# Roll stage of the third attention: norm's power for two batches, counts on VectorE and tags on ScalarE

## What is computed

```python
agg = jnp.einsum('bhekl,bk->bhel', gathered, tmp_corr)      # rolled values, weighted
out = agg.transpose(0, 3, 1, 2).reshape(Bq, Lq, Dq) @ Wo + bo
x = x + jnp.tanh(g_xattn[3]) * out
xn = _layernorm(x)                                           # (x - mean) / sqrt(var + 1e-5)
logits = jnp.einsum('bsh,eh->bse', xn, Wr)                   # 8 experts
top_v, top_i = jax.lax.top_k(jax.nn.softmax(logits), 2)      # two experts for each token
```

## Time and profile before

| | us |
|---|---|
| median of 3 runs | 1148.77 |
| lowest, highest | 1145.1, 1150.56 |
| the profiled run | 1153.46 |
| its span in the trace | 1151.7 |

### The profile page before, as it was taken

How to read it: one execution, slowest core, us unless ns; L and a number is a source line. 1 busy time by engine, 2 the same in 40 slices (tenths; PEclk the granted TensorE clock), 3 DMA queues, 4 the chain that set the end, 5 groups by cost and what they waited for, 6 DMA issues and landing times. The chain is left out here.

```text
span 1151.7 us, 21666 instructions
## 1 busy us (share of the span) xinstructions
PE 882.2 (77%) x6156; PEld 647.7 (56%) x6156; DVE 657.5 (57%) x1975; ACT 503.8 (44%) x1403; POOL 459.5 (40%) x835
## 2 busy tenths in 40 slices
PE   0799994788379999999649996799967727429992
PEld 0265663677247777777526775476655616317771
DVE  1588993434246777776533332799969715424443
ACT  0166662444036666655403332377842403115553
POOL 0345655245212344444332444343335406823434
PEclk9999996899569999999956555599986966559996
DMA  9990000122000000000011221100000220111214
GB/s 339 386 403 18 16 21 29 52 66 62 23 10 10 10 11 20 18 13 11 15 33 41 64 64 44 38 20 20 2 1 1 70 78 19 41 52 45 60 49 124
DMA packets 48930, 69.12 MB, mean 60 GB/s; under 512 B 7376, under 2 KB 38880, under 8 KB 48304
## 3 DMA queue, kind: packets, MB, share of 16 engines
q1 hardware_dynamic: 39824, 45.33, 12.0%
q0 software_dynamic: 7072, 14.69, 3.8%
q10 hardware_dynamic: 1920, 7.71, 1.8%
HBM read 31.48 MB, written 36.23 MB: 59 GB/s over the span
## 5 line engine op out<-in xcount | busy, mean ns | idle before, releaser
L1444 POOL DMA_INDIRECT expert_results<-block_out_f,block_to_f x125 | 120.7, 966 | 212.6 <-DVE block_out_f L1413 119.3
L1216 PE MATMUL banks<-weights_f,block_feat_f 128*128 x422 | 130.4, 439 | 2.9 <-ACT block_feat_f L1269 2.5
L309 POOL DMA_INDIRECT routed_region<-routed_lines,line_slots x96 | 96.3, 1003 | 23.2 <-issue 22.6
L245 POOL TENSOR_TENSOR small<-small,half_and_eps 128x1 f32<-128x1 f32 x160 | 91.6, 573 | 12.5
L1216 PEld LDWEIGHTS banks<-weights_f,block_feat_f 128*128 128x128 f32 x422 | 86.7, 259 | 8.8 <-issue 5.6
L861 PE MATMUL banks<-work_a,weights_a 128*128 128x128 f32 x512 | 78.3, 299 | 15.5 <-ACT work_a L1077 9.7
L744 ACT ACTIVATE probs_keymajor_a<-banks 128x512 f32<-128x512 f32 x128 | 70.2, 595 | 44.2 <-PE banks L549 44.2
L622 DVE TENSOR_REDUCE small<-banks 128x8 f32<-128x1024 f32 x64 | 77.6, 1212 | 7.0 <-PE banks L523 6.9
L861 PEld LDWEIGHTS banks<-work_a,weights_a 128*128 128x128 f32 x512 | 66.6, 203 | 25.9 <-ACT work_a L1077 13.5
L523 PE MATMUL banks<-work_a 32*128 32x512 f32 x256 | 80.8, 710 | 0.0
L631 DVE TENSOR_TENSOR exps_a<-banks,small 128x1024 f32<-128x1024 f32 x64 | 77.7, 1213 | 2.7 <-PE banks L549 2.4
(11 more groups left out here) (272 smaller groups left out, 2033.2 us busy)
## 6 DMA issues: line engine op xcount, KB each, us to landing
routed_region<-mid_a SPq DMA_DIRECT2D x34, 528.0 KB, 15.5
block_lines_f<-routed_region SPq DMA_DIRECT2D x125, 66.0 KB, 1.8
weights_f<-in_weights_f ACTq DMA_DIRECT2D x1, 4096.0 KB, 24.3
late_results<-expert_results SPq DMA_DIRECT2D x32, 128.0 KB, 2.0
weights_f<-in_weights_f SPq DMA_DIRECT2D x1, 3072.0 KB, 32.9
shifted_rows<-work_a SPq DMA_DIRECT2D x16, 128.0 KB, 1.7
both_outs_f<-expert_results SPq DMA_DIRECT2D x4, 512.0 KB, 5.6
expert_results<-block_out_f,block_to_f POOLq DMA_INDIRECT x125, 2.3
```

The costliest lines, as they stand in the source:

```text
L245: nc.gpsimd.tensor_tensor(rstd[:, s, 1:2], rstd[:, s, 0:1], k.half[:, 0:1], ALU.pow).then_inc(sem.rstd, 1)
L309: nc.gpsimd.indirect_dma_start(k.region, bass.IndirectOffsetOnAxis(k.slots[:, b, j:j + 1], 0), k.line[:, b % LINES, j, :], None).then_inc( ...
L1216: last = nc.tensor.matmul(bank[:, 2 + m % 2, i * hidden:(i + 1) * hidden], k.gotT[:, m % 2, :], tile[:, bass.ds(offs[m], hidden)], start=T ...
L1444: nc.gpsimd.indirect_dma_start(k.results, bass.IndirectOffsetOnAxis(k.to[:, m % RING:m % RING + 1], 0), k.y[:, m % RING, :], None).then_in ...
```

## The change

It touches `roll_block` alone, and there:

- eps is added on VectorE (`spread_out`, L1862 in the changed kernel), in the round and right behind the statistics;
- GpSimd raises to the power once for two batches (`deviations`, L1776, a tile of 128x2), at every even t, for batches t and t+1. Statistics have four places instead of two;
- the count is on VectorE (`counted`, L1871), last in the round;
- the tag copy is on ScalarE (`marked`, L1839), lag 3, last in the round;
- GpSimd's walk is the power (lag 0) and the send (lag 3 instead of 6).

```diff
-    stats, dev, norm = layer_norm_steps(nc, k, so, *norm_scratch(k.small, 0))
+    st, mv, rstd = split(k.small[:, 0:24], 6), split(k.small[:, 24:32], 2), split(k.small[:, 32:40], 2)
+    stats, dev, norm = layer_norm_steps(nc, k, so, st, mv, rstd)
...
+            def deviations(b, sl):
+                if b % 2 == 0:
+                    two = slice(b % 4, b % 4 + 2)
+                    wait(pool, so.var_eps, b + 2)
+                    wait(pool, s.xh2, b - 2)
+                    nc.gpsimd.tensor_tensor(rstd[:, two, 1:2], rstd[:, two, 0:1],
+                                            k.half[:, 0:1].unsqueeze(1).broadcast_to([T, 2, 1]), ALU.pow).then_inc(so.rstd, 2)
+
             begin(pool)
-            walk(pool, [(counted, 6), (sent, 6), (marked, 2), (dev_out, 0)])
+            walk(pool, [(deviations, 0), (sent, 3)])
...
-            walk(act, [(mirrored, 0), (next_T, 5), (logits, 6), (aggregated, 0)])
+            def marked(b, sl):
+                wait(act, s.marked, 1)
+                wait(act, ld.sent[b % LINES], lines_sent(2, b))
+                nc.scalar.activation(k.line[:, b % LINES, :, D:D + 1], k.marks[:, b, :].unsqueeze(2),
+                                     ACT.Copy).then_inc(s.tagged, 1)
+
+            walk(act, [(mirrored, 0), (next_T, 5), (logits, 6), (aggregated, 0), (marked, 3)])
...
+            def spread_out(b, sl):
+                wait(dve, so.stats, b + 1)
+                nc.vector.tensor_scalar(rstd[:, b % 4, 0:1], mv[:, b % 4, 1:2], EPS, None, ALU.add).then_inc(so.var_eps, 1)
...
+            def counted(b, sl):
+                wait(dve, s.marked, 3)
+                wait(dve, s.counted, b)
+                wait(dve, s.ranked, b + 1)
+                nc.vector.tensor_tensor(k.hist[:, :, 0:E3], k.hist[:, :, 0:E3], k.pick[:, sl, :, 0:E3],
+                                        ALU.add).then_inc(s.counted, 1)
...
-            walk(dve, [(norm_out, 3), (add, 0), (stats_out, 1), (chosen, 5), (placed, 6)])
+            walk(dve, [(norm_out, 3), (add, 0), (stats_out, 1), (spread_out, 1), (chosen, 5), (placed, 6), (counted, 6)])
```

More of the change, by code:

```diff
@@ L1846, in stats_out @@
                 wait(dve, s.added, b + 1)
-                stats(dve, at(k.x, b), sl, b + 1, s.xh2)
+                stats(dve, at(k.x, b), b % 4, b + 1, so.var_eps)
             def norm_out(b, sl):
                 line_free(dve, s, ld, 2, b)
-                norm(dve, k.line[:, b % LINES, :, 0:D], over(k.x[:, b, :], 2, 1), sl, b + 1).then_inc(s.xh2, 1)
+                norm(dve, k.line[:, b % LINES, :, 0:D], over(k.x[:, b, :], 2, 1), b % 4,
+                     b + 1).then_inc(s.xh2, 1)
+            def spread_out(b, sl):
+                wait(dve, so.stats, b + 1)
+                nc.vector.tensor_scalar(rstd[:, b % 4, 0:1], mv[:, b % 4, 1:2], EPS, None, ALU.add).then_inc(so.var_eps, 1)
             def chosen(b, sl):
                 choose(dve, b)
+            def counted(b, sl):
[4 more added lines that the diff above has]
+                                        ALU.add).then_inc(s.counted, 1)
             def placed(b, sl):
                 place(dve, b, bank[:, 5 - sl, 256:256 + E3])
-            walk(dve, [(norm_out, 3), (add, 0), (stats_out, 1), (chosen, 5), (placed, 6)])
+            walk(dve, [(norm_out, 3), (add, 0), (stats_out, 1), (spread_out, 1), (chosen, 5), (placed, 6), (counted, 6)])
 def flamingo_layers(nc, a, out, until=8):
```

## The result

The changed kernel took 1158.16 us (median of 4 runs, 1155.94 to 1160.08) against 1148.02 us for the kernel before beside it: 10.1 us or 0.9% slower, ratio 1.0089, 95% interval 1.0057 to 1.0120. The forecast was 1161.3 us, 12.5 above its median of before, with a range of 1154 to 1166. Direction and mechanism were right; the size was 2.4 us too large.

The account below looks back on a forecast made before the run. GpSimd's work was taken to set the roll stage's end; after the change, VectorE waits for powers queued behind sends. Rounds +8.4, tail +1.9 and start +2.2 make +12.5 on 1148.77: 1161.3 us, range 1154 to 1166.

Parts of the forecast that it names:

- The chain of two batches: Roll stage: power, VectorE's norm, slots and GpSimd's send wait in turn; 9.26 us per two batches against 7.46 before.
- VectorE's round with its data ready: Roll stage, after the power: norm 0.45, residual addition to slots 1.58, eps 0.2; 2.2 us claimed.
- the round through TensorE: Roll stage, VectorE's next round, which must go through TensorE: 3.0 us plus eps 0.2, 3.2 us claimed.
- The mis-sized term: Roll stage, from the slots to the even batch's first scatter on GpSimd: 0.76 us claimed, lower bound 0.41.
- the five rounds: Roll stage, sends 0 to 10: five rounds of two batches, 1.8 us more each, 0.6 less in the last; +8.4 us.
- the tail: Roll stage, last sends: send 11 waits for one more power, 5.2 us, then four steps of 2.6; +1.9 us.
- the start: Roll stage, up to send 0: first norms wait for the paired power, and send 0 starts 0.35 later; +2.2 us.
- The power of 128x2: GpSimd's power for two batches in the roll stage: 0.75 us, the middle between 0.57 and 0.95.
- What moved to VectorE and ScalarE: Roll stage: eps adds 0.2 us to VectorE's chain; count on VectorE and tag copy on ScalarE add nothing.
- The norm beside a scatter: Roll stage: a VectorE norm meeting a scatter's start adds up to 0.4 us in five rounds, 2 us; not summed.
- The cheap chain: Roll stage, same chain with power 0.57 and scatter start 0.41: +8.7 us, 1157.5 us; chance 0.20.
- The faster case: Roll stage: VectorE never finds the power missing, the VectorE-TensorE loop of 3.2 us bounds; -5.9 us, 1142.9; chance 0.08.

## Why the prediction was right, and where it was off

**What bounds before.** Right. GpSimd's sum set the step of 3.73, and taking the count away alone lowered it by 0.25.

**The chain of two batches.** Right in every link and in their order, as the alternation of 5.5 and 3.2 us between sends shows. The links as forecast and as measured: power 0.75 and 0.72; hand-over to the norm 0.05 and 0.14; VectorE's round with its data ready 2.2 and 2.12 (988.41 to 990.53); the round through TensorE 3.2 and 3.21; slots to the scatter 0.76 and 0.29; the send until the power 2.3 and 2.23. Sum 9.26 and 8.71.

**The mis-sized term** is the time from the slots to the first scatter. I had two bounds, 0.76 from 97 scatters of the expert stages and 0.41 from one of this stage, and took the 97 since GpSimd was idle ahead of them too. Measured was 0.29, below both. The 0.41 was no price of this step either: GpSimd's count ended only 0.18 us ahead of that send (962.62 + 0.22 to 963.01), so the send was held by its own engine. The likeness I chose by was the wrong one: what decides is not whether the engine is idle but whether the wait that is released last is also the last one in front of the scatter, as the exchange of waits shows in both directions. What the engine does in the other half microsecond no run shows. In the expert stage the result comes last and its wait is the last ahead of the scatter; in the roll stage the slots come last, but two more waits, already met, stand behind theirs. The term enters once in each of the five rounds, once in the tail and once at the start (there +0.35 forecast and -0.12 measured): 7 x 0.47 = 3.3 us of 3.4 too many (12.5 against the 9.08 to send 15). The other differences cancel: rounds and tail were each 0.2 us shorter than forecast without this term, the start 0.3 longer.

**The power of 128x2** took 0.72 against 0.57 for 128x1. So 0.15 of the 0.37 between an addition and a power comes again with the second column. The forecast's 0.75 was near, but by luck: no row spoke for the middle between 0.57 and 0.95.

**What moved to VectorE and ScalarE** cost what was said, 0.2 in each round for eps and nothing for count and tag: the second round takes 3.21. In the 5-round stretch no wait for a tag shows.

**The norm beside a scatter.** The prediction priced this at up to 0.4 us in each of five rounds, 2 us, and left it out of the sum. Here the first scatter of the odd send starts 0.21 us into a norm and takes 1.11 us; without a norm beside it, in the kernel with a power for each batch, the same place shows 1.03. The difference is 0.08 us for a norm of 0.41. In the run at lag 4 the scatter at 977.59 starts 0.06 us into a norm, lies beside more of it, and takes 1.03, nothing more. The Trainium skill, SBUF — State Buffer, section Who interferes with whom, says that a VectorE instruction in a 2-port mode blocks a GpSimd instruction fully until it ends. The times here are not those of a full block, nor is the power of the earlier trace rows, which starts 0.19 us into a norm of 0.41 and takes only 0.08 more than the mean; no row shows whether this norm runs in such a mode.

**Tail and start.** The tail was right but for the same term. The start's 1.99 us against 2.2 is partly luck: at the lower granted clock of the other profiles (0.70 against 0.82) the same code took 0.8 us longer to the slots of batch 0, and the forecast had no term for the clock. The 0.3 us behind the last send was not forecast: from the last scatter's end to the next matmul it is 2.96 us in the kernel before and with the count alone moved, 3.28 in those with the tag on ScalarE. What in the changed order makes it, no run separates.

**Rivals.** The cheap chain (1157.5) was nearer to the measured 1158.16 than the forecast, for half of its reason: the start of a scatter was cheap, the power was not. The faster case did not occur (its terms add up to 5.8 us less, not 5.9), and the reason given against it holds in the lag of 4, where the send is over when the norm is due and the step is the 3.2 us that it named.

## What to carry to other kernels

Work taken off the engine that sets the pace can lose time, when what stays on it moves behind something that another engine has only just released: look, for each result that others wait for, at what stands ahead of it in its own queue and when that can start. Here the same instructions gave 1169.9 or 1142.0 us by one digit in the order. When several waits stand ahead of an indirect DMA, try the one that is released last as the first of them.

## What the runs showed of the hardware

- An indirect DMA on GpSimd starts 0.28 to 0.29 us after the release when the last-released wait is not the last in front of it, 0.75 to 0.82 when it is; seen in both directions, at two places of the program.
- The two indirect DMAs of a send start 1.26 us apart (0.96 and 0.30) when a scatter stands right ahead of them and no norm runs beside them. Behind a power it is 1.34 (1.03 and 0.30), and up to 1.46 when a norm had started 0.17 to 0.27 us before the first of them.
- A power on GpSimd takes 0.57 us on 128x1 and 0.72 on 128x2; 0.65 to 0.69 on 128x1 when a norm on VectorE had started 0.15 to 0.20 us before it, but 0.57 when that was 0.05 or 0.09.
- The roll stage's start, behind 940 us of identical code, moved over 8.7 us between the profiled runs of eight kernels. A stage's length says more than its position.
- The length varies too: TensorE's mean granted clock up to send 0 was 0.70 to 0.82 in the changed kernel's order, and the same code took 0.8 us longer at 0.70 than at 0.82.
